# A two-block LoRA kernel: router logits and low-rank product computed apart for three of four token blocks, gates spread by DMA

## The reference

```python
logits = einsum('btd,ed->bte', x, Wr) + 5.0 * one_hot(language)[:, None]   # E = 8
topw, topi = top_k(logits, 2)
gates = sum(one_hot(topi, 8) * softmax(topw)[..., None], axis=-2)
h = einsum('btd,erd->bter', x, A)                                          # rank 16
x = x + einsum('btd,od->bto', x, W) + 2.0 * einsum('bter,bte,eor->bto', h, gates, B)
x = x + einsum('bnr,bor->bno', einsum('bni,bri->bnr', x, B1[adapter]), A1[adapter])
```

## Time and profile before

| | |
|---|---|
| time, median of 3 runs | 97.96 us (97.57 to 98.14) |
| the profiled execution's own time | 98.09 us |
| its span in the profile | 96.2 us, granted clock 0.992 |
| busy: TensorE, VectorE, ScalarE, GpSimd | 91.3, 60.4, 43.8, 36.6 us |
| down products of blocks 0, 1, 2 begin at | 26.71, 48.02, 69.41 us |

### The profile page before, as it was taken

The page is one execution under the profiler, slowest core; times in us unless marked ns, Lnnn a source line. Parts: engine busy times, 40 slices in busy tenths (PEclk is TensorE's granted clock), DMA queues, the critical chain, the costliest instruction groups (busy, mean ns, idle before and its releaser), DMA issues.

```text
span 96.2 us, 2162 instructions
## 1 busy us (share of the span) xinstructions
PE 91.3 (95%) x733; PEld 77.5 (81%) x733; DVE 60.4 (63%) x215; ACT 43.8 (46%) x88; POOL 36.6 (38%) x44
## 2 busy tenths in 40 slices
PE   4999999999999999999999999999999999999940
PEld 1499888889888897889888888889888888998940
DVE  4249799220699469860299379860399289863960
ACT  2570556629939960298028950497038500001100
POOL 5000767999521099991000099950000540000000
PEclk9999999999999999999999999999999999999996
DMA  1997987863915322798322224997000005050084
GB/s 21 363 325 194 329 328 174 266 174 66 354 58 131 76 49 65 201 374 218 72 48 50 46 57 127 383 238 286 9 0 3 7 0 214 4 218 0 7 267 169
DMA packets 14843, 14.36 MB, mean 149 GB/s; under 512 B 9968, under 2 KB 11248, under 8 KB 14448
## 3 DMA queue, kind: packets, MB, share of 16 engines
q1 hardware_dynamic: 13904, 11.85, 38.4%
q0 software_dynamic: 640, 2.10, 7.8%
q10 hardware_dynamic: 288, 0.28, 1.1%
HBM read 10.02 MB, written 4.19 MB: 148 GB/s over the span
## 4 chain that ended last, share of the span: by engine, by line
PE 92%; DVE 3%; DVEq 0%; issue 0%
PE main L653 15%; PE main L659 15%; PE main L665 15%; PE aw_ps L695 14%; PE side L747 6%; PE main L680 4%; PE main L679 4%; PE main L681 4%; PE aw_ps L771 3%; PE main L794 3%; PE side L695 3%; DVE xs L543 3%; PE side L727 2%; PE main L771 1%; PE side L771 1%; PE aw_ps L653 1%
## 5 line engine op out<-in xcount | busy, mean ns | idle before, releaser
L330 POOL TENSOR_TENSOR x_lo<-xs,x_hi 128x512 fp32r<-128x512 f32 x12 | 15.2, 1295 | 16.1 <-ACT x_hi L351 16.0
L653 PE MATMUL main<-x_hi,w_hi 128*128 128x512 f32 (+1 forms) x64 | 17.6, 397 | 0.0
L659 PE MATMUL main<-x_hi,w_lo 128*128 128x512 f32 (+1 forms) x64 | 16.9, 385 | 0.0
L665 PE MATMUL main<-x_lo,w_hi 128*128 128x512 f32 (+1 forms) x64 | 16.8, 384 | 0.0
L695 PE MATMUL aw_ps<-aws,xs 128*128 128x136 f32 x112 | 14.6, 284 | 0.0
L695 PEld LDWEIGHTS aw_ps<-aws,xs 128*128 128x128 f32 x112 | 14.2, 195 | 0.2
L659 PEld LDWEIGHTS main<-x_hi,w_lo 128*128 128x128 f32 x64 | 11.8, 188 | 2.6
L665 PEld LDWEIGHTS main<-x_lo,w_hi 128*128 128x128 f32 x64 | 11.8, 188 | 2.4
L653 PEld LDWEIGHTS main<-x_hi,w_hi 128*128 128x128 f32 x64 | 11.3, 188 | 2.2
L383 ACT ACTIVATE a_ops<-a_hi 64x512 fp32r<-64x512 f32 x12 | 7.6, 630 | 11.6 <-POOL a_rest L298 11.5
L502 DVE TENSOR_TENSOR xs<-main,xs 128x512 f32<-128x512 f32 x15 | 9.9, 684 | 2.1 <-PE main L681 2.1
(11 more groups left out here) (107 smaller groups left out, 134.8 us busy)
## 6 DMA issues: line engine op xcount, KB each, us to landing
out_t<-xs SPq DMA_DIRECT2D x16, 256.0 KB
xs<-x_t SPq DMA_DIRECT2D x3, 1024.0 KB, 4.7
b1s<-b_t SPq DMA_DIRECT2D x64, 32.0 KB, 1.9
xs<-x_t SPq DMA_DIRECT2D x4, 256.0 KB, 4.1
ws<-w_t SPq DMA_DIRECT2D x4, 256.0 KB, 4.8
b0s<-b_t SPq DMA_DIRECT2D x1, 256.0 KB, 5.2
aws<-aw_t ACTq DMA_DIRECT2D x1, 204.0 KB, 4.0
rows<-a_t,row_at POOLq DMA_INDIRECT x8, 3.9
```

The lines of the kernel that those rows point to most:

```text
L330: nc.gpsimd.tensor_tensor(x_lo[:, t % 2, c], xs[:, t, c], x_hi[:, t % 2, c].bitcast(F32), ALU.subtract).then_inc(x_lo_ready, 1)
L653: nc.tensor.matmul(out_ap, w_hi[:, c, k], x_hi[:, s, k, n], start=(k == 0), stop=False)
L659: nc.tensor.matmul(out_ap, w_lo[:, c, k], x_hi[:, s, k, n], start=False, stop=False)
L665: last = nc.tensor.matmul(out_ap, w_hi[:, c, k], x_lo[:, s, k, n], start=False, stop=False)
```

## The change

Block 0 stays as it is. For blocks u = 1, 2, 3:

- **Logits apart**: `logits_product(u)`, 16 float32 products with 32 columns of `aws` as weights (the last 8 of them the router's) and 128 tokens moving, tile j on columns 32j of the array, into `logits_bank` (`aw_ps1`). VectorE adds the bias to all of it and transposes in 32x32 blocks (`block_logits`), then as before.
- **h by rows**: `h_product(u)`, 12 products of 512 columns of `aw_hi`/`aw_lo` (split once, on ScalarE and VectorE) with `x_hi`/`x_lo`, into `h_bank` (`aw_ps0`); the output has experts x rank on the partitions, so no transpose on TensorE is needed. It stands where the transposes stood, behind base(u, 0).
- **Gates by DMA**: VectorE transposes the gates in 32x32 blocks into `gate_t`; SyncE writes them to DRAM (16 KB), waits, and reads them back with each expert's row on 16 partitions (`gate_rows`, 256 KB); VectorE multiplies `h_bank` by them in place (`gate_h_t`).
- The logits of u are made a stage earlier: those of block 1 behind base(0, 2), those of t+2 behind the down products of t. The gates of block 1 are made after the masks of block 0, those of t+2 after `gt_rest(t+1)`.
- SyncE's, GpSimd's and ScalarE's lists are reordered, as the diff shows. `up` uses the banks main2, main3, side0, side1, aw_ps1, aw_ps0, side0, side1.

```diff
...
-        up_banks = main[2:] + side[:1] + aw_ps + side[:1] + aw_ps
+        h_bank, logits_bank = aw_ps
+        up_banks = main[2:] + side + [logits_bank, h_bank] + side
         EARLY = 5
...
-            sp.wait_ge(clamped_ready, 1)
-            for t in range(NB):
-                if t == 1:
-                    sp.wait_ge(down_done, GPB)
-                for g in range(t * GPB, (t + 1) * GPB):
-                    load_b1(g)
-                if t + 2 < NB:
-                    sp.dma_start(xs[:, t + 2], x[:, t + 2]).then_inc(x_loaded[t + 2], 16)
-            for t in range(NB - 1):
+            def spread_gates(u):
+                sp.wait_ge(gate_t_ready, u)
+                sp.dma_start(gate_dram[u - 1].rearrange("e (q i) -> q e i", i=CW), gate_t[:, u - 1])\
+                  .then_inc(gate_written, 16)
+                sp.wait_ge(gate_written, 16 * u)
+                sp.dma_start(gate_rows[:, u - 1], gate_dram[u - 1].unsqueeze(1).broadcast_to([experts, rank, TB]))\
+                  .then_inc(gate_spread[u], 16)
...
+            sp.wait_ge(clamped_ready, 1)
+            load_b1(0)
+            sp.dma_start(xs[:, 2], x[:, 2]).then_inc(x_loaded[2], 16)
+            load_b1(1)
+            spread_gates(1)
+            sp.wait_ge(down_done, GPB)
+            load_b1(2)
+            load_b1(3)
+            sp.dma_start(xs[:, 3], x[:, 3]).then_inc(x_loaded[3], 16)
+            spread_gates(2)
+            load_b1(4)
+            load_b1(5)
+            store(0)
+            spread_gates(3)
+            load_b1(6)
+            load_b1(7)
+            store(1)
+            store(2)
...
+            pool.wait_ge(aw_lo_ready, 1)
+            x_rest(1, 0)
+            x_rest(1, 1)
+            split_a1(0)
+            split_a1(1)
+            x_rest(1, 2)
+            x_rest(1, 3)
+            pool.wait_ge(down_done, GPB)
+            gather(SLOTS)
+            for t in range(2, NB):
+                pool.wait_ge(gate_t_ready, t)
                 for g in range((t - 1) * GPB, t * GPB):
-                    if t > 1:
-                        split_a1(g)
-                    if g >= 1 and g - 1 + SLOTS < NG:
+                    split_a1(g)
+                for c in range(K):
+                    x_rest(t, c)
+                for g in range((t - 1) * GPB, t * GPB):
+                    if g - 1 + SLOTS < NG:
                         gather(g - 1 + SLOTS)
+            for g in range((NB - 1) * GPB, NG):
+                split_a1(g)
...
+            act.wait_ge(aw_loaded[0], 16)
+            act.wait_ge(aw_loaded[1], 16)
+            round_hi(aw_hi[:], aws[:, :, 0:H], aw_hi_ready)
...
+            exp_gap(1)
+            for g in range(GPB):
+                a1_half(g)
+            for g in range(GPB):
+                pack_a1(g)
             for t in range(NB - 1):
-                if t == 0:
-                    for g in range(GPB):
-                        a1_half(g)
-                    for g in range(GPB):
-                        pack_a1(g)
-                exp_gap(t + 1)
                 for g in range(t * GPB, (t + 1) * GPB):
                     down_half(g)
-                gt_half(t + 1)
+                if t + 2 < NB:
+                    exp_gap(t + 2)
                 for g in range((t + 1) * GPB, (t + 2) * GPB):
                     a1_half(g)
+                gt_half(t + 1)
...
+            def block_logits(u):
+                dve.wait_ge(logits_done, u)
+                nc.vector.scalar_tensor_tensor(
+                    logits_t[:], is_block_language[:, u - 1].unsqueeze(2).broadcast_to([P, TILES, CW]), LANG_BIAS,
+                    logits_bank[:, 0:P].rearrange("p (b i) -> p b i", b=TILES), ALU.mult, ALU.add)\
+                    .then_inc(logits_taken, 1)
+                dve.wait_ge(logits_taken, u)
+                then_wait(nc.vector.transpose(logits_b[:], logits_t[:]))
...
                 if u >= 1:
-                    dve.wait_ge(gt_done, u)
-                for j, h in h_parts(u):
+                    nc.vector.transpose(gate_t[:, u - 1], gate[:].rearrange("p b e -> p (b e)")).then_inc(
+                        gate_t_ready, 1)
...
+            def gate_h_t(u):
+                dve.wait_ge(h_done, u)
+                dve.wait_ge(gate_spread[u], 16)
+                nc.vector.tensor_tensor(h_bank[:], h_bank[:], gate_rows[:, u - 1], ALU.mult).then_inc(gated_t_ready, 1)
...
+            dve.wait_ge(aw_hi_ready, 1)
+            split_lo(aw_lo[:], aws[:, :, 0:H], aw_hi[:], aw_lo_ready)
+            block_logits(1)
+            top_two(logit_b)
             gt_rest(0)
+            pick(logit_b)
...
-                    if c == (K - 1 if t else 1) and more:
-                        top_two(t + 1)
                     if more or c < K - 1:
                         add_x1(t, c)
                 if more:
-                    pick()
                     for g in range(t * GPB, (t + 1) * GPB):
                         mask_down(g)
-                    gate_h(t + 1)
+                    if t == 0:
+                        gates(1)
+                    if t + 2 < NB:
+                        block_logits(t + 2)
+                        top_two(logit_b)
+                        pick(logit_b)
                     for g in range(t * GPB, (t + 1) * GPB):
                         down_rest(g)
+                    gate_h_t(t + 1)
                     gt_rest(t + 1)
+                    if t + 2 < NB:
+                        gates(t + 2)
                     for i in range(0, EARLY, 2):
                         add_x2(t, range(i, min(i + 2, EARLY)))
...
+            def logits_product(u):
+                pe.wait_ge(x_loaded[u], 16)
+                if u == 1:
+                    pe.wait_ge(gated_ready, 2)
+                elif u == 2:
+                    pe.wait_ge(logits_taken, 1)
+                else:
+                    pe.wait_ge(x2_ready, (u - 3) * PARTS + up_banks.index(logits_bank) + 1)
+                for k in range(K):
                     for j in range(TILES):
-                        last = aw_product(0, j, k)
-                last.then_inc(aw_done, 1)
-            def aw_tiles(u):
-                pe.wait_ge(x_loaded[u], 16)
-                pe.wait_ge(gated_ready, u * 2)
-                if u >= 2:
-                    pe.wait_ge(x2_ready, (u - 1) * PARTS)
-                for j in range(TILES):
-                    for k in range(K):
-                        last = aw_product(u, j, k)
-                last.then_inc(aw_done, 1)
-            def gt_transposes(u):
-                pe.wait_ge(gated_ready, u * 2 + 1)
-                if u == 0:
-                    pe.wait_ge(const_ready, 3)
+                        last = nc.tensor.matmul(logits_bank[j * CW:(j + 1) * CW, 0:P], aws[:, k, AWN - CW:AWN],
+                                                xs[:, u, k, j * P:(j + 1) * P], start=(k == 0), stop=(k == K - 1),
+                                                tile_position=(0, j * CW))
+                last.then_inc(logits_done, 1)
+            def h_product(u):
+                s = u % 2
+                pe.wait_ge(aw_hi_ready, 1)
+                pe.wait_ge(aw_lo_ready, 1)
+                if u == 1:
+                    pe.wait_ge(gated_ready, 2)
                 else:
-                    pe.wait_ge(down_ready, u * GPB)
+                    pe.wait_ge(x2_ready, (u - 2) * PARTS + up_banks.index(h_bank) + 1)
+                for k in range(K):
+                    nc.tensor.matmul(h_bank[:], aw_hi[:, k], x_hi[:, s, k], start=(k == 0), stop=False)
+                for k in range(K):
+                    nc.tensor.matmul(h_bank[:], aw_lo[:, k], x_hi[:, s, k], start=False, stop=False)
+                for k in range(K):
+                    last = nc.tensor.matmul(h_bank[:], aw_hi[:, k], x_lo[:, s, k], start=False, stop=(k == K - 1))
+                last.then_inc(h_done, 1)
...
-                if i >= EARLY:
+                if bank is logits_bank:
+                    pe.wait_ge(logits_taken, min(t + 2, NB - 1))
+                if bank is h_bank:
+                    pe.wait_ge(gt_lo_ready, t + 2)
+                if up_banks.index(bank) < i:
                     pe.wait_ge(x2_ready, t * PARTS + up_banks.index(bank) + 1)
...
             base(0, 0)
             base(0, 1)
             base(0, 2)
-            gt_transposes(0)
+            logits_product(1)
+            gt_transposes()
             base(0, 3)
             for c in range(K):
-                if c == 1:
-                    aw_tiles(1)
                 lora(0, c)
...
                 down_part(t * GPB + 1, K - 1)
+                if t + 2 < NB:
+                    logits_product(t + 2)
                 base(t + 1, 0)
-                gt_transposes(t + 1)
+                h_product(t + 1)
                 base(t + 1, 1)
                 for i in range(EARLY):
                     up(t, i)
                 lora(t + 1, 2)
                 if t + 2 < NB:
                     base(t + 1, 3)
-                    aw_tiles(t + 2)
```

(17 more changed lines are left out.)

132 lines of the change are left out of this document (76 added, 56 removed).

## The result

The changed kernel takes 100.11 us (median of 6 runs, 99.03 to 100.33) beside 97.81 for the kernel before on the same chip: 1.022 times as long, interval 1.017 to 1.027. The forecast was 97.7 us with 99.0 as its upper end. Ratios are those of the record, which leave out runs over 1.5% above the fastest of their kernel; the medians keep them, so that the two can differ by up to 0.5%.

A forecast was written before the change was run, and what follows sets the result against it. TensorE was taken as the bound in every stage but the last 4 us. Its work at -1.24 us plus waits of 0.8 and 0.2 gave -0.24, so 97.85 profiled and 97.7 us as median; range 96.6 to 99.0.

The forecast's parts named there:

- TensorE's work: TensorE instructions removed and added over all blocks: -1.24 us in all, if nothing waits.
- D: Rival, logits on TensorE: column tiles don't run side by side with 128 columns; logits 3.4 us, time 105; chance 0.04.
- The first stretch: TensorE in block 0 up to its down products: -3.70 + 1.00 + 0.23 = -2.47 us.
- the last at +1.9: TensorE from the down products of block 2 to the end: -0.46 + 2.73 - 0.09 = +2.18 us.
- First wait: Block 0's down products wait for b1 rows of the second group, landing at 25.1: 0.8 us, from 0 to 1.6.
- Second wait: Block 1's base column 2 waits because gates come by DMA write and read: 0.2 us, from 0 to 1.4.
- D + 7.3: Gate rows of block 1 ready for VectorE's product 7.3 us after the end of block 0's down products.
- rival C: Block 1's gate rows late: slower by 0.5% once that wait passes 0.93 us, 99.6 at upper ends; chance 0.20.
- A: The forecast case: part of the gain eaten by short waits, time 97.2 to 98.4 us; chance 0.44.
- The sign that was to point to C: VectorE waiting for the gate rows for over 1 us before its product.
- Between down products 1 and 2: TensorE from block 1's down products to block 2's: -0.43 - 0.09 = -0.52 us, no hole expected.
- Edits with cover: Reordered or added work on ScalarE, VectorE, GpSimd and SyncE falls in idle time or meets its deadlines: no cost.

## Why the prediction was wrong

**TensorE's work: right.** The logits take 1.01 (16.76 to 17.77) where 1.00 was taken, h 2.80 (31.46 to 34.26) for 2.73. Logits of 1.01 and not 3.4 mean that the column tiles do run side by side with 128 columns, so D was rightly kept small. The first stretch came out at -2.44 for -2.47, the last at +1.9 for +2.18.

**First wait: the step that failed most.** The prediction took b1's landing from the old row, 1.6 to 2.8 us, and let the 1 MB in front cost "a few tenths": a landing at 25.1, a wait of 0.8, 1.6 at most. The issue of the last copy was right (22.75; 22.9 measured). The landing was the term that failed: 2.35 us were taken for it, and it took 3.7, so that it came at 26.6 and TensorE waited for over 2 us. The prediction had the trace's load of the engines (0.77) and treated the copies as work that shares a pool that is through near 23.5. The engines were in fact little used from 24 us on (0.27), and the copy still came late. The upper bound of 2.8 us was a row of copies that had nothing large ahead of them; behind the 1 MB each took 3.2 to 5.8. With the 1 MB out of the way the down products ran without a wait, so the cause is shown; how a large load delays small copies issued behind it isn't.

**Second wait: right in kind, short in size.** The product came at D + 8.1 (27.57 to 35.63) for D + 7.3: the write 2.2 for 2.0, the read 3.9 for 3.2. The wait was 0.45 to 0.6 for 0.2, inside the bounds. Reading from 16 rows takes some 0.5 off the read. The wait does not reach the 0.93 that rival C wanted: the kernel became slower by A's first wait grown beyond its bound, and not by C's mechanism. The sign that was to point to C is nevertheless there: VectorE waits 2.77 us for the gate rows before its product. It was a bad sign: VectorE comes to this product early, and only what passes TensorE's deadline costs time, here 0.45 to 0.6 of the 2.77. Rivals A and C both held the first wait at 0.8; that is why only C's upper end came near 100.

**Between down products 1 and 2: a wait not seen at all.** -0.52 was predicted and +0.41 measured; hole 3 is nearly all of these 0.93 (2.03 - 1.15 = 0.88). The prediction said of GpSimd's list "covered", and costed its order only by whether the results come in time. Where in TensorE's work the gathers fall was not asked, so this term stood at nothing.

**Edits with cover.** The transposes on VectorE take 0.31 and 0.21 where 0.25 and 0.15 were taken. That small operations of the router stand behind GpSimd's long ones (0.85 for 0.17) was not counted; in the changed kernel it is hidden by hole 1, and it comes out once hole 1 is gone.

The sum, redone: -1.24, and waits of 2.05 to 2.2, 0.5 to 0.6 and 0.6 to 0.9, give +1.9 to +2.5 against +2.3 of span measured. The mechanism of faster TensorE work was real: with holes 1 and 3 out of the way and hole 2 down to 0.19, the kernel is faster than before by 0.5 to 0.8%.

## What to carry to other kernels

Shortening the bound engine's work brings every later transfer's deadline nearer: list the loads that the shorter stretch needs and price each with what is queued ahead of it, not with an old row of copies that had nothing large ahead of them. A large load goes where nothing small is behind it that is needed soon, here to the very front. When a list on GpSimd is reordered, look also at which TensorE work its gathers fall beside, and at the small VectorE operations that fall beside its long ones.

## What the runs showed of the hardware

- Copies of 32 KB issued right behind a 1 MB load in one queue land after 3.2 to 5.8 us (2.0 to 5.8 over five profiles), and after 1.6 to 3.1 without it (both other load orders). SyncE also issues the last of them later, at 22.9 instead of 21.3 and 21.5.
- A 256 KB read from DRAM that spreads 8 rows over 128 partitions takes 3.65 to 4.34 us from issue to use (fourteen profiles); with every row there twice, so that the source has 16, it takes 3.17 to 3.46 (three).
- 100 waits that are fulfilled already, at the head of TensorE's list, start its work some 5 us later (9.14 for 4.05, both on chip 9).
- A VectorE operation of 4 values per partition lasts until GpSimd's running one is done: 1.28 us for 0.16, and 0.85 for 0.17.
- Row gathers that fall beside the down products or the logits (64 down records in the 1.15 us from 46.73 to 47.88, one every 18 ns) go with a pause of TensorE with no wait in its list: 0.36 to 0.63 us of idle time beside the down products, 0.20 to 0.33 at a time beside the logits. The first pause begins within 0.2 us of the end of a gather on GpSimd. Gathers that end beside products of 512 columns have none.
- It shows in the changed kernel's first profile and in all eight on chips 9 and 8 that have the gathers there, and in none of four on chip 1. By what path a gather does it, and why one chip is spared, stays open; the position in the instruction list, a fetch of instructions at that time and the read of the gates are ruled out by the runs above.
